# One maximum over three score banks in place of three maxima in a ring, in a cross-attention and mixture-of-experts kernel

## The reference

```python
q = rope(q_in @ Wq + bq); k = rope(k_in @ Wk + bk); v = v_in @ Wv + bv
scores = einsum('bhqd,bhkd->bhqk', q, k) / sqrt(64)
scores = where(arange(sk) < lengths, scores, -inf)
out = einsum('bhqk,bhkd->bhqd', softmax(scores), v)
x = x + out @ Wo + bo
x = x + mixture(layernorm(x))      # 8 experts of width 512, top 2
```

## Time and profile before

| | |
|---|---|
| median of 3 runs | 1301.48 us (1300.73 to 1307.26) |
| profiled execution: its time, its span | 1301.48 us, 1299.6 us |
| PE busy | 1074.6 us (83% of the span) |
| DVE busy | 1010.8 us (78%) |
| ACT busy | 639.0 us (49%) |
| POOL busy | 661.3 us (51%) |
| mean granted TensorE clock | 0.938 |

### The profile page before, as it was taken

One profiled execution on the slowest core, in us unless ns is written; L12 is line 12 of the kernel. 1 busy time (PEld: TensorE's weight loads), 2 busy tenths in 40 slices (PEclk: granted clock), 3 DMA queues, 4 the chain that ended last, 5 costly groups with the idle time before them and its releaser, 6 DMA issues. The chain is left out here.

```text
span 1299.6 us, 32397 instructions
## 1 busy us (share of the span) xinstructions
PE 1074.6 (83%) x12780; PEld 713.4 (55%) x12966; DVE 1010.8 (78%) x1760; ACT 639.0 (49%) x1196; POOL 661.3 (51%) x472
## 2 busy tenths in 40 slices
PE   1556989989988998998998999899968842999992
PEld 0322556556656655655665665566647741666661
DVE  5736999899899999989989999999838761444445
ACT  3523555655555565655555556555536530333330
POOL 0053683584476477367448547733337647322213
PEclk9657999999999999999999999999979866999997
DMA  7034121421412322152141242212049603211134
GB/s 261 9 69 113 43 53 39 120 54 38 126 36 60 84 74 56 33 132 54 26 126 40 60 110 51 61 35 54 14 162 334 229 9 122 78 59 58 62 109 152
DMA packets 92509, 110.56 MB, mean 85 GB/s; under 512 B 44701, under 2 KB 72286, under 8 KB 92094
## 3 DMA queue, kind: packets, MB, share of 16 engines
q1 hardware_dynamic: 81390, 80.53, 23.9%
q10 hardware_dynamic: 7552, 18.51, 4.2%
q0 software_dynamic: 3408, 9.33, 2.0%
HBM read 43.63 MB, written 25.33 MB: 53 GB/s over the span
## 5 line engine op out<-in xcount | busy, mean ns | idle before, releaser
L802 DVE TENSOR_REDUCE part_max<-mx 128x1 f32<-128x427 f32 x768 | 420.1, 592 | 55.8 <-PE mx L582 54.7
L707 ACT ACTIVATE prob<-sc 128x512 f32<-128x512 f32 x640 | 347.7, 595 | 186.4 <-PE sc L570 182.7
L902 POOL TENSOR_TENSOR prob_lo<-prob 128x1024 bf16<-128x1024 f32 x128 | 249.2, 1947 | 253.8 <-ACT prob L707 253.8
L611 PE MATMUL pv<-VV,prob_lo 128*128 128x65 bf16 x2560 | 269.7, 195 | 0.0
L609 PE MATMUL pv<-VV,prob 128*128 128x65 bf16 x2560 | 268.4, 193 | 0.8 <-POOL prob_lo L902 0.6
L610 PE MATMUL pv<-VV,prob 128*128 128x64 bf16 x2560 | 268.5, 193 | 0.0
L814 DVE TENSOR_TENSOR prob_lo<-prob 128x1024 bf16<-128x1024 f32 x192 | 260.6, 1357 | 6.5 <-ACT prob L707 6.5
L582 PE MATMUL mx<-K,Q 128*128 128x427 bf16 x768 | 238.2, 350 | 28.0 <-DVE part_max L802 17.2
L609 PEld LDWEIGHTS pv<-VV,prob 128*128 128x128 bf16 x2560 | 240.5, 99 | 31.5 <-POOL prob_lo L902 0.7
L610 PEld LDWEIGHTS pv<-VV,prob 128*128 128x128 bf16 x2560 | 237.8, 97 | 27.2
L570 PE MATMUL sc<-Q,K 65*128 65x512 bf16 x640 | 243.7, 381 | 10.4 <-issue 4.0
(11 more groups left out here) (187 smaller groups left out, 1836.2 us busy)
## 6 DMA issues: line engine op xcount, KB each, us to landing
we<-in_w_exp ACTq DMA_DIRECT2D x16, 768.0 KB, 6.3
q32s<-q SPq DMA_DIRECT2D x128, 64.0 KB, 2.0
Q<-next_q_hi SPq DMA_DIRECT2D x32, 256.0 KB, 3.7
attention_out<-o_out SPq DMA_DIRECT2D x64, 128.0 KB, 2.0
o_in<-attention_out SPq DMA_DIRECT2D x16, 512.0 KB, 5.4
expert_inputs<-zeros SPq DMA_DIRECT2D x7, 771.0 KB, 6.0
VV<-next_v SPq DMA_DIRECT2D x16, 322.5 KB, 3.6
q32s<-q SPq DMA_DIRECT2D x128, 40.0 KB, 1.9
```

Source lines behind the costliest of these rows:

```text
L611: ins = pe.matmul(out, prob_lo[:, s % PRING, j, qt * P:(qt + 1) * P], VV[a][:, t, HD:VW], start=False, stop=t == pl.kt - 1, skip_group_che ...
L707: act.activation(prob[:, s % PRING, j, :], sc[n % 2][:], ACT.Exp, scale=HD ** -0.5).then_inc(exp_done, 1)
L802: dve.tensor_reduce(part_max[:, b_ % 2, qt, h:h + 1], mx[:, pl.part_banks(qt, h)[0]:pl.part_banks(qt, h)[-1] + 1, 0:pl.width], mybir.AxisL ...
L902: pool.tensor_tensor(prob_lo[:, s % PRING, 0:g, :], prob[:, s % PRING, 0:g, :], hi_half(prob[:, s % PRING, 0:g, :])[:, :, 1::2], ALU.subtr ...
```

## The change

In the branch for up to 12 key tiles the three stretches of a query tile become one part with three sub-stretches, and there is one part in flight in place of three. TensorE issues the three matmuls of a query tile together, and VectorE takes one maximum of 3 x 427 elements over the three banks. A block has 4 parts in place of 12. By lines 79 to 82 they fall on the slots m = 3, 4, 0, 1, 2 as 1, 1, 1, 1, 0. Since slot m = 2 has no part, the second edit lets TensorE do that slot's scores where no part leads.

```diff
         if kt * P <= 3 * 512:
             self.width = -(-kt * P // 3)
-            self.parts = [[min(j * self.width, kt * P - self.width)] for j in range(3)]
-            self.part_slots = 3
+            self.parts = [[min(j * self.width, kt * P - self.width) for j in range(3)]]
+            self.part_slots = 1
...
-                        behind = pl.row_block(s) is not None
+                        behind = pl.row_block(s) is not None or not pl.parts_of(s)
                         if behind:
                             slot_scores(p, s, last)
```

## The result

| | before | after |
|---|---|---|
| median | 1301.45 us (1300.73 to 1307.26) | 1398.96 us (1398.26 to 1401.6) |
| ratio, 95% interval | | 1.0743 [1.0724, 1.0761] |
| span of the profiled execution | 1299.6 us | 1397.3 us |
| DVE busy | 1010.8 us | 989.6 us |
| mean granted TensorE clock | 0.938 | 0.945 |

The change makes the kernel 97.5 us slower. The direction was forecast (0.92), the size was not: 56 us were expected, and 1398.96 lies above the range of 1325 to 1388.

A forecast was written before the change was run, and what follows sets the result against it. TensorE's issue bounded cycles without projection, VectorE cycles 3 to 5. Seven head pairs at +6.3 us (+44), the last pair +9 and the opening +2.5 gave +56 on 1301.48: 1357 us, range 1325 to 1388.

The forecast's parts named there:

- The rival in which each bank pays a start: The merged VectorE reduction takes 1.78 us, lengthening most cycles' first two legs: 1408 us in all, chance 0.07.
- a turn of 2.27 us: From a tile's first part matmul through VectorE's reduction until TensorE resumes: 2.27 us, against 2.14 of TensorE work per slot.
- the walked cycle: A block cycle without projection, from one m = 3 part to the next: 12.23 us, against 10.88 before.
- The last pair's +9: Eighth head pair, without projections: seven cycles with parts, each 1.33 us longer, +9 us.
- the opening's +2.5: Start of `attend`, where TensorE and VectorE do only parts: four turns for 12 steps of 0.51 us, +2.5 us.
- Cycles 2, 3 and 7: Three of a head pair's eight block cycles, with projections: forecast 15.2, 15.6 and 12.3 us.
- the last leg of cycles 4, 5 and 6: From slot 1's part to the next m = 3 part, in cycles with projections: 5.86, 5.86 and 6.95 us.
- TensorE, not VectorE, closes the cycle: In cycles 3 to 5 TensorE ends the cycle, so VectorE's saving there is not collected.
- the wait for the column falls to little: TensorE's wait for VectorE's column of maxima should fall from 36 us to little.
- VectorE bound, faster: If turns fit between TensorE's visits, only VectorE's saving counts: 1260 us everywhere, 1288 in cycles 3 to 5; chance 0.05.
- cancel: Loss and gain offset each other over the whole kernel, within 0.5% of 1301 us; chance 0.03.
- Only some cycles pay: Cycles 2 to 6 keep their old length, those without much rotary work grow: 3.0 us per pair, 1334 us; chance 0.20.

The follow-up runs named there:

- e1: Changed kernel with three reductions of 427 per tile again, still one tile in flight: 1420.7 us.
- e3: Changed kernel whose one reduction reads only 3 x 213 of the 3 x 427 columns: 1341.7 us.
- e11: Changed kernel with the column of maxima taken in slot m = 1, right behind the last reduction: 1400.4 us.
- e14: Changed kernel with ScalarE's copy of the row put ahead of the high half and evacuation, column left in place: 1423.7 us.
- e13: Changed kernel with both the column in slot m = 1 and ScalarE's row copy taken ahead: 1429.1 us.
- e17: Changed kernel with column and row taken ahead (e13) and GpSimd's low halves cut to 64 columns: 1354.0 us.
- e4: Changed kernel with GpSimd's low halves cut from 512 to 64 columns per key tile: 1351.2 us.
- e5: Kernel before with GpSimd's low halves cut from 512 to 64 columns per key tile: 1264.95 us.
- e6: Changed kernel with VectorE's reciprocal moved from slot m = 1 to slot m = 2, behind the column: 1407.7 us.
- e16: Two-part, scores-first kernel (e10) with ScalarE's copy of the row taken ahead: 1325.3 us.
- e7: Changed kernel with TensorE doing the scores ahead of the part in every slot: 1321.1 us.
- e10: Tile in two parts (two banks, then one), two in flight, scores ahead of all parts: 1302.7 us.
- e2: Kernel before with two banks in flight in place of three, no instruction changed: 1370.4 us.
- e9: Tile in two parts (two banks, then one), two in flight, without scores first in every slot: 1353.1 us.
- e18: Two-part, scores-first kernel (e10) with the single bank first and the two banks behind it: 1323.8 us.

## Why the prediction was wrong in size

**The reduction.** Forecast 1.48 us, measured 1.488 with bounds of 1.43 and 1.78. The rival in which each bank pays a start (1408 us) lies nearest to the measured time, and is wrong all the same: L802 did not take the 1.78 us that it needs. By the formula of the Trainium skill, "VectorE: DVE Perf Modes", section "The TRN2 errata", an estimate is (120 + 1281) / 0.96 = 1460 ns for the one, which the trace bears out within 2%, and 1.71 us for three, where e1 shows 1.62: the part of it that the neighbours' overlap takes away was rightly left out.

**One part in flight.** Forecast a turn of 2.27 us, measured 2.30; the walked cycle 12.23, measured 12.42. The wait for L802 before L582 went from 44 to 119 us, just short of the "over 120". The last pair's +9 came out as +10.8, the opening's +2.5 as +3.2; by the prediction's own terms, four turns of 2.27 for 12 steps of 0.51, it should have been +3.0. e3 shows that the turn is the cause in these cycles, e1 that the merging is not. Cycles 2, 3 and 7 were within 0.3 us of the forecast.

**The step that failed** is the last leg of cycles 4, 5 and 6, and with it "TensorE, not VectorE, closes the cycle" and "the wait for the column falls to little". The leg was put at 5.86 us in cycles 4 and 5, counting TensorE's instructions alone; it measured 7.02 and 6.91. In cycle 6 it measured 8.40, for 6.95 forecast, and the first leg 6.15 for 5.66. These three cycles miss by 1.07, 0.85 and 1.96 us, 3.9 of a pair's 4.7, and the pairs are 35 of the 42 us by which the sum was short. The column wait fell from 35.8 only to 19.7 us.

What the walk left out is the rotary work behind slot 1 and what hangs on it. It let the column follow the reduction, where the code has the reciprocal and the rotary work of the unit between them: in cycle 4, 0.54 us of waiting and 2.42 of work (766.03 to 768.45). It put ScalarE's queue ahead of the row at 0.1 to 0.25 us, where the high half waits for the same rotary work. In cycle 6 it did count rotary work, 1.99 us ahead of the second V unit; there the reciprocal's wait of 0.53 us and 2.70 us of work stood (798.95 to 801.65). Each of the two holds the leg: in cycle 4 it stays at 7.02 with the column alone ahead (e11), is 6.59 with the row alone ahead (e14), and with both ahead 5.98 (e13), or 5.87 with GpSimd cut (e17), the forecast value.

The walk also took the durations of the rotary work from before. A two-input VectorE operation had no fixed duration in these traces: behind slot 1 it took 1.55, 0.70 and 1.38 us in before and 1.89, 1.97 and 1.92 in after, and in cycle 6 L788 behind m = 3 took 2.06 for 1.55, which is the first leg's miss. With GpSimd's low halves cut the last legs are within 0.25 us of the forecast (e4). That cycle 5's first leg came out right, 6.40 forecast and 6.35 measured, is luck: before had 1.72 us in L774 and 0.55 in L788 there, after has 0.15 and 2.02. The Trainium skill, "SBUF — State Buffer", section "Who interferes with whom", says that a VectorE instruction with two SBUF inputs contends with a GpSimd instruction that reads SBUF and that `tensor_reduce` never does on this chip. The traces agree on both: L788 goes from 566 ns with GpSimd cut to 1813 in after, L802 (which reads PSUM) stays at 1488 in both.

**How much of the miss is which.** The last legs of cycles 4 to 6 hold 3.66 us of the pair's 4.7, by an estimate from this one pair 26 of the 42 us, and 3.15 of the 3.66 go with GpSimd's low halves. Against the kernel before, the same low halves account for only some 11 us (e4 and e5), because before pays for them too, in operations that the walk did not count. The other legs and cycles miss by some 1 us a pair, the last pair and the opening by 2.5 together. The 4.4 us behind the last column stay open; as other runs vary by more there, they may be nothing that the change did. Taking column and row ahead gives nothing in the end, since the time comes back in the first two legs (e13, e17); what brings it back in e17, without GpSimd's low halves, was not followed. That the chain from VectorE's rotary work over ScalarE's high half and evacuation to the row, to TensorE's next part and projection, and back to VectorE closes as a loop is argued, not shown. e6 and e14 to e16 can't help here, since their granted clock fell.

**The rivals.** "VectorE bound, faster" and "cancel" are out: VectorE's reductions took 39 us less, in e3 210 us less, and the kernel stayed slower than before both times. "Only some cycles pay" is out: all eight cycles pay, the third by 1.48 us and the sixth by most. For cycles 4 to 6 the rise is 1.28, 0.72 and 2.91, where I had forecast 0.2, -0.1 and 0.95.

**What sets the price** only showed behind the prediction. e7 gives 78 of the 97.5 us back with one tile in flight, one reduction, and an unchanged turn. So the loss depends on where the parts stand as well as on the turn: in after the parts of slots 3 and 4 have 0.7 us of other TensorE work between them and need 1.7. I had walked exactly this 1.00 us wait and treated it as a term of the sum, not as something that the order could remove.

## What to carry to other kernels

Merging instructions over the banks of a ring takes the ring away: reckon the producer-consumer turn (here 2.3 us) against the producer's other work between two visits, slot by slot, and put other work between the visits (e7) or keep two parts in flight (e10) before counting the saving. Two in flight are no guarantee: two thirds of a tile lost 69 us (e2), and e9 with the old order 52. When a wait grows on the busiest engine, walk the queue of every engine up to the next hand-over, not only that of the engine that was the bound, and take durations of two-input VectorE work as a range that depends on what GpSimd does beside it. A wait removed by taking one hand-over ahead came back elsewhere here (e11, e17); moving the producer's other work between its visits paid (e7). Before calling a reordering bad, look at the granted clock: it fell in e6, e13 to e16 and e18.

## What the runs showed of the hardware

- A VectorE maximum over three PSUM banks in one instruction costs nothing per bank: 1488 ns for 1281 elements, 819 for 639. That is 1.04 ns per element between them and some 150 ns besides; at the same 1.04 the 592 ns of 427 elements in one bank leave 147.
- The granted clock can be lost to short standstills in a busy stage. In e13 it is at 0.50 behind standstills of 2.08 us (above), in e18 also behind one of 1.62 us for the column:

```profile
496.41 0.38 PE L592 MATMUL mx<-ident_b,max_col 128*1 128x128 bf16 x4 [1.62 <-DVE max_col L810]
498.00:500.00 2.00, 2.00 (x27) 1.62 (x26) 2.00 (x4) 0.52 (x2) 1.82 (x3) 0.50 0.26 62
```

  In after, TensorE stands for 1.7 us seven times (waits above), and from 130 us on no part of `attend` is below 1.00. So the length of one standstill does not decide it; what does was not tried.
- L788 took from 547 ns (e5) to 1829 ns (e3) with the same operands. Its time in a trace of before says little about its time in a changed order.
